# Causal attention block of a decoder layer: the output product as three float32r products with Wo's parts streamed from DRAM, and the set-up block dissolved into the first steps

## The reference, cut to what matters

```python
xn = (x - mu) * rsqrt(var + EPS) * gamma           # x is itself layer-normed first
q = (xn @ Wq).reshape(b, n, 16, 128)               # 16 query heads of 128
k, v = (xn @ Wkv)[..., :128], (xn @ Wkv)[..., 128:]
q, k = rotary(q) * 128 ** -0.5, rotary(k)
attn = softmax(where(causal, -inf, q @ k.T))
x = x + (attn @ v).reshape(b, n, 2048) @ Wo        # Wo: 2048 x 512, float32
```

## Time and profile before

| | us |
|---|---|
| median of 3 runs | 1276.69 (1276.41 to 1286.49) |
| profiled execution | 1278.61 |
| its span | 1276.8 |
| PE, DVE, ACT, POOL busy | 1067.3, 887.9, 557.0, 522.7 |
| attention | from about 39 to 663 |
| cross attention and feed-forward | from about 664 to the end |

### The profile page before, as it was taken

How to read it: one execution, slowest core, us unless ns; L and a number is a source line. 1 busy time by engine, 2 the same in 40 slices (tenths; PEclk the granted TensorE clock), 3 DMA queues, 4 the chain that set the end, 5 groups by cost and what they waited for, 6 DMA issues and landing times. The chain is left out here.

```text
span 1276.8 us, 24901 instructions
## 1 busy us (share of the span) xinstructions
PE 1067.3 (84%) x9332; PEld 724.5 (57%) x9348; DVE 887.9 (70%) x1715; ACT 557.0 (44%) x899; POOL 522.7 (41%) x462
## 2 busy tenths in 40 slices
PE   0689999999999999999863888988898973766775
PEld 0667677676777767677521565656666641333332
DVE  5667777767777777778832567666767653888884
ACT  3144333333333333334511366666656551555553
POOL 3343434434343443434424134343333334566653
PEclk9999999999999999999985799999999985899998
DMA  8321000000000000001205566757665410000000
GB/s 311 131 71 66 1 1 1 1 2 0 0 0 0 1 0 0 0 0 48 67 23 123 124 169 145 182 139 182 144 167 127 95 27 31 9 25 25 25 25 25
DMA packets 39007, 80.19 MB, mean 63 GB/s; under 512 B 8896, under 2 KB 21696, under 8 KB 35328
## 3 DMA queue, kind: packets, MB, share of 16 engines
q1 hardware_dynamic: 36112, 71.46, 21.4%
q10 hardware_dynamic: 2208, 4.59, 1.0%
q0 software_dynamic: 592, 2.89, 0.6%
HBM read 61.74 MB, written 16.78 MB: 61 GB/s over the span
## 5 line engine op out<-in xcount | busy, mean ns | idle before, releaser
L408 PE MATMUL Yb<-Wo,a_oN 128*128 128x512 f32 x512 | 232.7, 598 | 0.0
L1071 DVE TENSOR_REDUCE mx<-Sm 128x4 f32<-128x768 f32 x128 | 122.4, 957 | 86.4 <-PE Sm L811 85.8
L506 POOL TENSOR_TENSOR a_ql<-a_rot,a_qh 128x512 fp32r<-128x512 f32 x64 | 83.8, 1313 | 182.0 <-ACT a_qh L463 182.0
L408 PEld LDWEIGHTS Yb<-Wo,a_oN 128*128 128x128 f32 x512 | 97.6, 192 | 99.3 <-issue 94.2
L909 ACT ACTIVATE x_ex<-Se 128x768 f32<-128x768 f32 x128 | 103.1, 806 | 116.0 <-PE Se L811 116.0
L341 PE MATMUL Qb<-a_xTh,WqH 128*128 128x256 f32 x512 | 146.0, 285 | 2.4 <-DVE a_vl L607 2.4
L455 ACT ACTIVATE Lb<-Lb 128x512 f32<-128x512 f32 x64 | 37.2, 582 | 250.2 <-PE Ob L400 250.2
L342 PE MATMUL Qb<-a_xTl,WqH 128*128 128x256 f32 x512 | 144.9, 283 | 0.0
L343 PE MATMUL Qb<-a_xTh,WqL 128*128 128x256 f32 x512 | 144.8, 283 | 0.0
L513 POOL TENSOR_TENSOR a_pl<-a_pr,a_ph 128x512 fp32r<-128x512 f32 x64 | 83.4, 1304 | 120.7 <-ACT a_ph L450 120.7
L569 DVE TRANSPOSE_TENSOR_REDUCE a_rmax<-Sb 128x16 f32<-128x512 f32 x64 | 45.9, 717 | 81.9 <-PE Sb L382 81.3
(11 more groups left out here) (189 smaller groups left out, 2483.3 us busy)
## 6 DMA issues: line engine op xcount, KB each, us to landing
K<-k_parts SPq DMA_DIRECT2D x32, 256.0 KB, 4.6
q_parts<-x_qp SPq DMA_DIRECT2D x16, 384.0 KB, 3.0
Q<-q_parts SPq DMA_DIRECT2D x16, 384.0 KB, 5.6
k_parts<-x_kp SPq DMA_DIRECT2D x16, 384.0 KB, 7.3
a_w_stage<-in_gateT SPq DMA_DIRECT2D x8, 704.0 KB, 4.0
x_w_stage<-in_gateT SPq DMA_DIRECT2D x8, 704.0 KB, 5.3
X<-in_x SPq DMA_DIRECT2D x4, 1024.0 KB, 16.2
Wo<-in_Wo ACTq DMA_DIRECT2D x1, 4096.0 KB, 13.9
```

What stands on the lines that cost most here:

```text
L408: mm = pe.matmul(Yb[s % 2][:, :], oN[:, s % 2, i * P:(i + 1) * P], t["Wo"][:, HG * u + i, :], start=(i == 0), stop=(i == HG - 1))
L506: pool.tensor_tensor(rot_dst(False, True, par, r), rbuf(par, r)[:, 0:rot_width(r)], rot_dst(True, False, par, r).bitcast(F32), ALU.subtrac ...
L1071: dve.tensor_reduce(mx[:, half, at:at + 4].rearrange("p (j a) -> p j a", j=2), Sm[:, :, 0:2 * WIN].rearrange("p j (a c) -> p j a c", a=2), ...
```

## The change

**The product.** `out_projection` becomes three float32r matmuls for each head: oH x WoH, oH x WoL, oL x WoH. For it ScalarE rounds oN to oH (`outputs_high`, at the end of each step), and GpSimd writes oL = oN - oH (`outputs_low`, at the start of the next).

**Wo.** SBUF has no room for both parts of all of Wo. Two slots hold the parts of two head sets (4 heads, 2 x 1 MB each). In group 0 SP loads plain Wo for head set u into slot u % 2, ScalarE writes WoH, GpSimd WoL (head by head), and SP writes both to a DRAM tensor `wo_parts` (`keep`). From group 1 on GpSimd issues the loads of the parts from there (`out_weights_again`, two DMAs of 1 MB, 128 rows of 8 KB, in each even step), between `outputs_low` and pl.

**The set-up.** `setup_attention` is gone. SP's queue starts with two batches of X, Wkv and the constants, then Wq in four column blocks (2 KB rows) with the other batches between, then Wo. ScalarE writes the high parts as its entries in the first steps; for head pairs 2 to 7 it first scales Wq in place (four operations), then rounds. The low parts of Wkv and of pairs 0 and 1 stay with VectorE, those of pairs 2 to 7 go to GpSimd (`query_weights_low`). Statistics and norm scales are made in three runs of batches (0 and 1, 2 to 7, 8 to 15). Low parts (WqL, WkvL, pl, oL, WoL) lie in the same memory as the plain tensors they come from.

**Feed-forward pieces.** The twelve pieces are summed in group 0 at steps 3 to 6 (four) and in group 7 at each of the 8 steps.

```diff
-                    mm = pe.matmul(Yb[s % 2][:, :], oN[:, s % 2, i * P:(i + 1) * P], t["Wo"][:, HG * u + i, :],
-                                   start=(i == 0), stop=(i == HG - 1))
+                    high, low = oH[:, s % 2, i * P:(i + 1) * P], oL[:, s % 2, i * P:(i + 1) * P]
+                    pe.matmul(Yb[s % 2][:, :], high, WoH[u % 2][:, i, :], start=(i == 0), stop=False)
+                    pe.matmul(Yb[s % 2][:, :], high, WoL[u % 2][:, i, :], start=False, stop=False)
+                    mm = pe.matmul(Yb[s % 2][:, :], low, WoH[u % 2][:, i, :], start=False, stop=(i == HG - 1))
...
+            def outputs_high(g, s):
+                act.wait_ge(oN_ready, done(g, STEPS, s, ON0))
+                act.activation(oH[:, s % 2, :], oN[:, s % 2, :], ACT.Copy).then_inc(oH_ready, 1)
...
+                if isinstance(g, int) and (g, s) == (-1, STEPS - 3):
+                    first_query_weights_high()
+                    query_weights_high(2)
+                    masks()
+                    query_weights_high(3)
+                if isinstance(g, int) and (g, s) == (-1, STEPS - 2):
+                    query_weights_high(4)
...
+                if isinstance(g, int) and (g, s) == (-1, STEPS - 1):
+                    query_weights_high(5)
+                    query_weights_high(6)
+                if first and s == 0:
+                    query_weights_high(7)
+                if first and s in (1, 2, 5, 6):
+                    out_weights_high((0, 1, 2, 3)[(1, 2, 5, 6).index(s)])
+                if real(pg):
+                    outputs_high(pg, ps)
...
+            rows(0)
+            sp.dma_start(Wkv[:, :, :], dram["Wkv"].rearrange("(k p) n -> p k n", p=P)).then_inc(wkv_in, 16)
+            for name in ("ident", "cos", "sinS"):
+                sp.dma_start(t[name][:, :], dram[name]).then_inc(consts_in, 16)
+            query_weights(0)
+            sp.dma_start(causal[:, :], dram["causal"]).then_inc(masks_in, 16)
+            query_weights(1)
+            rows(1)
+            query_weights(2)
+            query_weights(3)
+            rows(2)
+            out_weights(0)
+            out_weights(1)
...
+            keep(0)
+            summed(0)
+            keep(1)
...
+            def out_weights_again(g, u):
+
+                pool.wait_ge(wo_kept[u], 32)
+                pool.wait_ge(wo_kept[(u + 2) % U], 32)
+                pool.wait_ge(y_full, done(g, STEPS, NG * u + NG - 1, Y0))
+                pool.sem_inc(slot_free, 1)
+                for part, dst in ((0, WoH), (1, WoL)):
+                    pool.dma_start(dst[u % 2][:, :, :].rearrange("p h n -> p (h n)"),
+                                   wo_parts[(u + 2) % U, part].bitcast(F32R)).then_inc(wo_in[u % 2], 16)
+
+            def outputs_low(g, s):
+                pool.wait_ge(oH_ready, done(g, STEPS, s))
+                pool.tensor_tensor(oL[:, s % 2, :], oN[:, s % 2, :], oH[:, s % 2, :].bitcast(F32), ALU.subtract).then_inc(oL_ready, 1)
...
             def step(g, par, s):
+                og, os = before(g, s, 2)
+                if real(og):
+                    outputs_low(og, os)
+                wg, ws = before(g, s, 4)
+                if real(wg) and ws % NG == 0:
+                    u = ws // NG
+                    if not isinstance(wg, int) or 0 < wg < G - 1 or wg == G - 1 and u < U - 2:
+                        out_weights_again(wg, u)
+                first = isinstance(g, int) and g == 0
+                if isinstance(g, int) and (g, s) == (-1, 0):
+                    power(0, 0)
+                    power(0, 1)
+                if isinstance(g, int) and (g, s) == (-1, STEPS - 3):
+                    power(1, 0)
+                    query_weights_low(2)
+                if first and s in (4, STEPS - 2):
+                    out_weights_low(1 if s == 4 else 2, (2, 3))
+                if first and s == 2:
+                    out_weights_low(0, (2, 3))
                 pg, ps = before(g, s, 1)
                 if real(pg):
                     pool.wait_ge(ph_ready, done(pg, STEPS, ps))
                     pool.tensor_tensor(pl[:, :], pr[:, :], ph[:, :].bitcast(F32), ALU.subtract).then_inc(pl_ready, 1)
...
+                if isinstance(g, int) and (g, s) == (-1, STEPS - 2):
+                    query_weights_low(3)
                 for pair_g, pair_par, m in pairs_at(g, par, s):
                     rotated_low(pair_g, pair_par, 1 + m)
+                if isinstance(g, int) and (g, s) == (-1, STEPS - 1):
+                    power(1, 1)
+                    query_weights_low(4)
+                if first and s == 0:
+                    query_weights_low(5)
+                    query_weights_low(6)
+                if first and s == 1:
+                    query_weights_low(7)
+                    out_weights_low(0, (0, 1))
+                if first and s == 3:
+                    out_weights_low(1, (0, 1))
+                    power(2, 0)
+                if first and s == 4:
+                    power(2, 1)
+                if first and s == STEPS - 3:
+                    out_weights_low(2, (0, 1))
+                if first and s == STEPS - 1:
+                    out_weights_low(3, (2, 3))
```

More of the change, by code:

```diff
@@ L107, in norm_scales @@
     return gpsimd_part, vector_part
[L110 to L200, removed]
@@ L203, in attention, with plain_and_rounded @@
+def plain_and_rounded(nc, ctx, name, shape):
+    with nc.sbuf_tensor(f"{name}_plain", shape, F32) as plain:
+        pass
+    return plain, ctx.enter_context(nc.sbuf_tensor(name, shape, F32R))
 def attention(nc, t, dram):
@@ L300, in summed_at @@
         def summed_at(g, s):
-            first = len(PIECES) // 2
-            if isinstance(g, int) and g in (0, G - 1) and s < first:
-                return [s + (first if g else 0)]
+            if isinstance(g, int) and g == 0 and 3 <= s < 3 + SUMMED_FIRST:
+                return [s - 3]
+            if isinstance(g, int) and g == G - 1:
+                return [SUMMED_FIRST + s]
             return []
@@ L330, in transposes @@
             def transposes(g, par):
+                if isinstance(g, int) and g == 0:
+                    pe.wait_ge(consts_in, 16 * 3)
                 for j in range(NG):
@@ L362, in project_pair @@
                 n = NG + 1 + m
+                if isinstance(g, int) and g == 0:
+                    if m < 2:
+                        pe.wait_ge(wq0_low, KD)
+                    else:
+                        pe.wait_ge(wq_low, m - 1)
                 pe.wait_ge(q_free, free(g, USES, n))
@@ L493, in _, with rows, query_weights, out_weights @@
         def _(sp):
-            for n in range(len(PIECES)):
+            def rows(i):
+                lo, hi = X_RUNS[i]
+                sp.dma_start(t["X"][:, lo:hi, :], dram["x"][lo:hi].rearrange("b t d -> t b d")).then_inc(x_in[i], 16)
+            def query_weights(c):
+                sp.dma_start(Wq[:, :, c * D:(c + 1) * D],
+                             dram["Wq"][:, c * D:(c + 1) * D].rearrange("(k p) n -> p k n", p=P)).then_inc(wq_in[c], 16)
+            def out_weights(u):
+                sp.dma_start(WoLp[u % 2][:, :, :],
+                             dram["Wo"][u * HG * P:(u + 1) * HG * P, :].rearrange("(h p) n -> p h n", p=P)).then_inc(wo_raw[u % 2], 16)
+            def keep(u):
+                sp.wait_ge(wo_low, HG * (u + 1))
+                for part, src in ((0, WoH), (1, WoL)):
+                    sp.dma_start(wo_parts[u, part], src[u % 2][:, :, :].rearrange("p h n -> p (h n)").bitcast(F32)).then_inc(wo_kept[u], 16)
+            def slot_read(g, u):
+                sp.wait_ge(y_full, done(g, STEPS, NG * u + NG - 1, Y0))
+            def summed(n):
                 if n > 0:
@@ new lines, in _ @@
+            query_weights(3)
[5 more added lines that the diff above has]
+            keep(1)
+            slot_read(0, 0)
+            sp.wait_ge(wo_kept[0], 32)
+            out_weights(2)
+            summed(1)
+            summed(2)
+            slot_read(0, 1)
+            sp.wait_ge(wo_kept[1], 32)
+            out_weights(3)
+            summed(3)
+            keep(2)
+            summed(4)
+            keep(3)
@@ L499, in _, with power @@
+            for n in range(5, len(PIECES)):
+                summed(n)
         @block.gpsimd
         def _(pool):
+            pool.memset(t["half"][:, :], -0.5).then_inc(const_set, 1)
+            pool.memset(Dg[:, :].bitcast(F32), 0.0).then_inc(const_set, 1)
+            pool.wait_ge(const_set, 2)
             pool.sem_inc(dg_ready, DG0)
             pool.sem_inc(ql_ready, QL0)
+            def power(i, n):
+                lo, hi = X_RUNS[i]
+                pool.wait_ge(norm_step, 5 * i + (1, 4)[n])
+                pool.tensor_tensor(t[("r1", "r2")[n]][:, lo:hi], t["ve"][:, lo:hi], t["half"][:, 0:1].to_broadcast([P, hi - lo]),
+                                   ALU.pow).then_inc(pow_done, 1)
@@ L611, in step @@
                     add_to_x(pg, ps)
```

(2 more changed lines are left out.)

181 lines of the change are left out of this document (163 added, 18 removed).

## The result

| | before | after |
|---|---|---|
| median of 4 runs | 1278.9 | 1313.55 (1310.18 to 1316.65) |
| profiled execution | 1278.61 | 1311.79 |
| its span | 1276.8 | 1310.0 |

A forecast was written before the change was run, and what follows sets the result against it. TensorE was taken to bound attention. Gains of 18.1 - 2 + 11.5 + 1 = 28.6 us off the profiled 1278.61 gave 1250.0, 1248.1 for the median, rounded up to 1249; own range 1232 to 1264.

The forecast's parts named there:

- The product: In each of 64 attention steps, 12 float32r matmuls take 2.79 us for 3.43; 41 us gained if everything new stays hidden.
- The issues: In even steps GpSimd's two DMA issues, 1.09 us, stand between oL and pl and stall TensorE 1.05 us.
- An odd step just fits: In odd steps pl ends at 10.63 us and TensorE asks at 10.68: no stall, a step of 7.98.
- The copies beside the issues: VectorE's four copies, 1.56 us beside GpSimd for 0.94 without, share something with it; 2 us taken for group 0.
- The stream: Loads of two parts, 2 MB every two steps, need some 7 to 14 us of 18 allowed: hidden.
- The front: Before attention's steps: first `scores` at 30.5 us, 29.2 earlier; first `values` at 45.7, 27.0 earlier.
- Group 0: GpSimd's 70 us of work there gives back part of the early start, leaving 18.1 us ahead where group 1 begins.
- The tail: In group 7's last steps shorter products gain, eight pieces to sum eat slack: -2 to 3 us, taken as 1 gained.
- (b): Rival: issues and VectorE's copies exclude each other, about 1.0 us later in three steps of seven groups: 1270; chance 0.20.
- (c): Rival: a pair of GpSimd's DMA issues costs over 2.5 us; at 3.7 the time is 1304 us; chance 0.10.
- (d): Rival: the stream is late, each us beyond 18 for 2 MB costs 28; at 20 us 1305; chance 0.03.

The follow-up runs named there:

- the dissolved set-up alone: The kernel after with Wo resident in plain float32 and the old product (no oH, oL, parts of Wo, `keep` or stream): 1263.07 us, 0.985 of before.

## Why the prediction was wrong, step by step

- **The product**: right. 2.79 forecast, 2.76 measured.
- **The issues**: right. 1.09 for the pair, 0.59 + 0.54 measured; stall of 1.05 in even steps, 8.99 - 7.95 = 1.04 once the copies were elsewhere. The pair's effect on the loop was missed: moving it alone gave 2%.
- **"An odd step just fits"**: this is the step that failed. It took the copies' end at S+2.34 and ql's start at S+6.73 from the rows of before, and followed ql, oL, pl forward from there. But oL and pl now stand where the copies run, hold two or three of them, and so move the copies' end, the rotation behind it and the next ql. Following the copies' end once round gives 8.47 to 8.60, over 7.98; measured, shift to shift, 8.4 to 9.0 in odd steps and 9.5 to 9.7 in even ones, for 7.98 and 9.03. A slack of 0.05 us was a warning too. In groups 1 to 6 some 20 us were lost where 11.5 were to be gained.
- **"The copies beside the issues"**: the 1.56 beside pl against 0.94 alone was seen and called shared, then priced in one direction (GpSimd's issues waiting for VectorE), and as a term for group 0 of 0 to 0.6 a meeting. In the rows the copies are the ones that wait, one for each GpSimd subtraction that they meet: in the two steps shown 1.5 and 2.05 us over the 1.56 of before. No issue took over 0.76 us. The section of the Trainium skill that the prediction cites (SBUF — State Buffer, Who interferes with whom) says both directions; I used one.
- **The stream**: right, hidden. The two loads landed 5.1 and 7.2 us after their issue for 18 allowed.

```profile
a_WoH<-wo_parts POOLq DMA_DIRECT2D x28, 1024.0 KB, 5.1
a_WoL<-wo_parts POOLq DMA_DIRECT2D x28, 1024.0 KB, 7.2
```

- **The front**: nearly right. First `scores` 26.8 earlier for 29.2, first `values` 24.2 for 27.0.
- **Group 0**: mis-sized. `values` of steps 1, 2, 3 and 7 at 58.7, 67.0, 78.5, 119.6 forecast, at 65.1, 74.8, 89.6, 142.6 measured: a lead of 18.1 turned into -4.9. This is a second term that failed, 23 of the 62 us between forecast and result. The working had GpSimd over 90% busy and setting the pace; it was busy 66%. VectorE's instructions were held here too. The longest, the write of a scale 6 columns wide, took 6.37 us, until GpSimd's two WqL parts and pl were through:

```profile
42.14 6.37 DVE L707 TENSOR_TENSOR scale<-r 128x6 f32<-128x6 f32 x1
```
```profile
42.53 4.73 POOL L582 TENSOR_TENSOR WqL<-WqL_plain,WqH 128x1024 fp32r<-128x1024 f32 x2
47.23 1.25 POOL L633 TENSOR_TENSOR a_pr<-a_pr_plain,a_ph 128x512 fp32r<-128x512 f32 x1
```

  But the same write took the same 6.37 us in the dissolved set-up alone, whose group 0 is 25 us shorter, and with the copies on ScalarE it took 0.34 and group 0 stayed as long. So held operations are not what group 0 lost. PE waited up to 7.6 us for pl there, and in such waits the granted clock fell and stayed low for some us after: a mean of 0.83 from 50 to 100 us, 0.97 in the kernel with the float32 product, so part of the stretch ran at the lower of the two levels (1.2 of 2.4 GHz). `keep` was said to have no one waiting but SP; ScalarE waited 5.3 us behind it, and taking that wait away gained nothing that can be measured. What the runs show is that the 25 us go when the parts of Wo and of the outputs go; how they split between the longer chain through ScalarE and GpSimd and the clock stays open.
- **The tail**: +1 forecast; measured some 5.7 lost, the 7.2 from the middle of group 6 less that group's 1.5. TensorE's last three waits for pl are 5.5, 4.3 and 2.7 us, where the last three of the kernel before are 3.7, 1.8 and 2.7; no run took it apart.
- **The rivals**: (b) was the nearest by its mechanism, since it had copies and GpSimd exclude each other, but from the wrong side and at 1.0 us a step; its 1270 missed by 44. (c) and (d) had sums of 1304 and 1305, nearer in number, but by causes that did not happen: a pair of issues took 1.13 us, and the loads landed in time.

## What to carry to other kernels

Before adding work to an engine at 40%, look for short operations of another engine that run longer beside it than alone, look at them one by one, and count how many of the new instructions each could meet. Then close the loop: follow one instruction's end round to its own next end, and compare that with the bound engine's step; a step that "just fits" from a fixed start doesn't show this. And price a part's one-off preparation against its steady saving (19 us against 3.7 a group): with eight groups it came to nothing. Last, when a cure brings less than expected, ask which stretch it left unchanged: here that took the held copies out of the account of group 0.

## What the runs showed of the hardware

Four 32x16 fp32 copies on VectorE took 0.94 us alone (0.16 to 0.17 each, 0.03 between) and 1.56 where pl alone stood beside them. Where GpSimd had several 128x512 subtractions without a gap, they took 2.07 us when they began 2.1 us into the run of 3.79, 3.04 when they began 1.0 into it, and 3.61 with two DMA issues in the run. ScalarE's took 0.93 in the same place.

The merged rows read as if four copies waited for a whole run of GpSimd instructions. The single ones say otherwise: from 200 to 600 us of the kernel after, 77 copies took over 0.25 us, each had one GpSimd instruction on tiles to wait out, and each ended 0.02 to 0.04 after it. They slip in between, but one at a time, and the next is held again; so what a row of tiny copies pays is set by how many of them there are and how many GpSimd instructions are left. With the issues in the run it was longer for one of them: a copy that began during the first issue (314.77) ended at 316.92, behind the second issue and pl.

```profile
313.50 1.05 DVE L764 COPY a_mparts<-a_rmax 32x16 f32<-32x16 f32 x1
314.58 0.16 DVE L764 COPY a_mparts<-a_rmax 32x16 f32<-32x16 f32 x1
314.77 2.14 DVE L764 COPY a_mparts<-a_rmax 32x16 f32<-32x16 f32 x1
316.95 0.17 DVE L764 COPY a_mparts<-a_rmax 32x16 f32<-32x16 f32 x1
```

The 6.37 us of the scale's write, through three GpSimd instructions, is the case that doesn't fit one hold for each instruction, and no run explains it. And one idle operation of 1.28 us on GpSimd cost nothing that can be measured where two cost 4.2%.
